# Decoder layer: low halves of wz in the last attention group made by GpSimd, x2 sums moved up on VectorE

## What is computed

```
b_att = softmax(max(s, axis=2), axis=1)
q2c_att = einsum('bc,bcd->bd', b_att, c)[:, None, :]
x = concatenate([c, c2q_att, c * c2q_att, c * q2c_att], axis=-1)
z = x @ W_l.T + b_l
```

## Time and profile before

| what | number |
|---|---|
| median of 3 runs | 656.0 us |
| profiled execution, its own time | 655.94 us |
| its span in the profile | 654.1 us |
| PE busy | 645.0 us (99%) |
| DVE busy | 470.1 us (72%) |
| ACT busy | 329.7 us (50%) |
| POOL busy | 241.3 us (37%) |
| mean granted clock of TensorE | 1.0 |

### The profile page before, as it was taken

One profiled execution on the slowest core, in us unless ns is written; L12 is line 12 of the kernel. 1 busy time (PEld: TensorE's weight loads), 2 busy tenths in 40 slices (PEclk: granted clock), 3 DMA queues, 4 the chain that ended last, 5 costly groups with the idle time before them and its releaser, 6 DMA issues. The chain is left out here.

```text
span 654.1 us, 11891 instructions
## 1 busy us (share of the span) xinstructions
PE 645.0 (99%) x3922; PEld 551.8 (84%) x3922; DVE 470.1 (72%) x1259; ACT 329.7 (50%) x779; POOL 241.3 (37%) x305
## 2 busy tenths in 40 slices
PE   8999999999999999999999989999999999999997
PEld 5878888889788888897897878888888888888887
DVE  5788868878788788787888978676575765747433
ACT  4575675555756755556576454333533344334331
POOL 2256163353562633534644233223232232322221
PEclk9999999999999999999999999999999999999999
DMA  8534044051340440513624260403214033230300
GB/s 232 155 97 144 8 124 122 28 168 48 92 145 7 122 122 25 165 54 87 197 71 125 84 220 21 180 27 130 98 52 174 0 129 96 70 125 1 151 13 32
DMA packets 51806, 64.44 MB, mean 99 GB/s; under 512 B 3944, under 2 KB 49560, under 8 KB 50880
## 3 DMA queue, kind: packets, MB, share of 16 engines
q1 hardware_dynamic: 51776, 64.06, 31.5%
HBM read 56.60 MB, written 7.45 MB: 98 GB/s over the span
## 5 line engine op out<-in xcount | busy, mean ns | idle before, releaser
L1630 POOL TENSOR_TENSOR xt<-xt,cw_wide 128x512 f32<-128x512 f32 x55 | 72.5, 1318 | 187.2 <-ACT xt L1587 187.2
L1654 DVE TENSOR_TENSOR res<-bank,xt 128x512 f32<-128x512 f32 x62 | 42.6, 688 | 62.3 <-POOL xt L1630 58.3
L1591 ACT ACTIVATE a_hi<-res 128x512 fp32r<-128x512 f32 x42 | 26.7, 635 | 82.4 <-DVE res L1654 82.4
L75 PE MATMUL bank<-h_hi,w_lo 128*128 128x512 f32 x168 | 67.1, 400 | 0.1
L76 PE MATMUL bank<-h_lo,w_hi 128*128 128x512 f32 x168 | 65.9, 392 | 0.0
L77 PE MATMUL bank<-h_hi,w_hi 128*128 128x512 f32 x168 | 65.6, 390 | 0.0
L1025 POOL TENSOR_TENSOR wz_lo<-tmp,wz_hi 128x512 fp32r<-128x512 f32 x28 | 34.9, 1284 | 37.6 <-DVE tmp L1196 37.6
L643 PE MATMUL bank<-cw_wide,ctw 128*112 128x375 f32 x128 | 46.7, 486 | 0.4
L656 PE MATMUL bank<-ctxf,qg 125*112 125x256 f32 x192 | 46.7, 379 | 0.0
L1659 DVE TENSOR_TENSOR a_lo<-res,a_hi 128x512 fp32r<-128x512 f32 x42 | 30.0, 714 | 22.4 <-ACT a_hi L1591 22.4
L1587 ACT ACTIVATE xt<-bank 128x512 f32<-128x512 f32 x61 | 36.0, 590 | 14.6 <-PE bank L77 14.5
(11 more groups left out here) (241 smaller groups left out, 2016.1 us busy)
## 6 DMA issues: line engine op xcount, KB each, us to landing
cw_wide<-in_ctx_t SPq DMA_DIRECT2D x32, 375.0 KB
ctxf<-in_ctx SPq DMA_DIRECT2D x32, 375.0 KB
cw_wide<-cw_scratch SPq DMA_DIRECT2D x7, 1536.0 KB, 7.5
xt<-in_x SPq DMA_DIRECT2D x8, 448.0 KB, 3.9
x_scratch<-x2b SPq DMA_DIRECT2D x8, 448.0 KB, 3.2
x2n<-x_scratch SPq DMA_DIRECT2D x7, 512.0 KB, 4.6
cw_wide<-cw_scratch SPq DMA_DIRECT2D x7, 512.0 KB, 4.2
x2t<-x_scratch SPq DMA_DIRECT2D x7, 512.0 KB, 3.9
```

Source lines behind the costliest of these rows:

```text
L75: pe.matmul(dst, a_lo, b_hi, start=first, stop=False, **kw)
L1591: act.activation(a_hi[n % (AHEAD + 1)][:, :], af[(p + n) % 2][:, :], ACT.Copy).then_inc(a_hi_ok, 1)
L1630: pool.tensor_tensor(sg[b][:, :], sg[b][:, :], cw_wide[p][:, ORDER[n], :], ALU.mult).then_inc(sgw_ok, 1)
L1654: dve.tensor_tensor(af[b][:, :], u_bank[b][:, :], sg[b][:, :], ALU.mult).then_inc(af_ok, 1)
```

## The change

In the last attention group the four subtractions `wz_lo[j] = wz[j] - wz_hi[j]` go from VectorE to GpSimd. GpSimd makes each as soon as its high half is there, without waiting for all sums, and ahead of the weighting of `sg[1]`; the wait for `wz_lo_ok` falls away there, since GpSimd itself has made them. VectorE runs its four sums in a row, then the low half `op_lo0`, and then the two x2 sums; before, `op_lo0` stood behind the x2 sums.

```
@@ GpSimd, group @@
                     if last:
+                        for j in range(G):
+                            pool.wait_ge(wz_hi_ok, ev[j])
+                            pool.tensor_tensor(wz_lo[:, j, :, :], wz[:, j, :, :], f32(wz_hi[:, j, :, :]), ALU.subtract).then_inc(wz_lo_ok, 1)
                         pool.wait_ge(sg_ok, 2)
                         pool.wait_ge(cw_in, 16)
-                        pool.wait_ge(wz_lo_ok, ev[G - 1])
                         pool.tensor_tensor(sg[1][:, :], sg[1][:, :], cw_wide0[:, 0, :], ALU.mult).then_inc(sgw_ok, 1)
@@ VectorE, group @@
-                    def wz_low_last(j):
-                        dve.wait_ge(wz_hi_ok, ev[j])
-                        dve.tensor_tensor(wz_lo[:, j, :, :], wz[:, j, :, :], f32(wz_hi[:, j, :, :]), ALU.subtract).then_inc(wz_lo_ok, 1)
...
-                        wz_sum(0)
-                        wz_sum(1)
-                        wz_low_last(0)
-                        wz_sum(2)
-                        wz_low_last(1)
-                        wz_sum(3)
-                        wz_low_last(2)
-                        wz_low_last(3)
+                        for j in range(G):
+                            wz_sum(j)
+                        dve.wait_ge(a_hi_ok, 1)
+                        dve.tensor_tensor(op_lo0[:, :], af[0][:, :], f32(op_hi0[:, :]), ALU.subtract).then_inc(a_lo_ok, 1)
                         x2_sum(i, 0)
                         x2_sum(i, 1)
-                        dve.wait_ge(a_hi_ok, 1)
-                        dve.tensor_tensor(op_lo0[:, :], af[0][:, :], f32(op_hi0[:, :]), ALU.subtract).then_inc(a_lo_ok, 1)
```

## The result

The changed kernel takes 658.0 us (median of 10 runs), the one before 656.19 (10 runs beside it): ratio 1.0031, 95% interval 1.0022 to 1.0039. It is slower by 1.8 us; 658.2 was forecast. The profiled execution took 658.32 us, with a span of 656.5 against 654.1.

A forecast was written before the change was run, and what follows sets the result against it. The engines' meeting between the blocks, which VectorE reaches last, was taken as the bound. With turns VectorE arrives at 377.83 + 1.82 = 379.65 against 377.47, +2.2 us; 656.0 + 2.2 = 658.2, range 657.4 to 659.2.

The forecast's parts named there:

- The bound and the meeting: Between the two blocks, VectorE reaches the engines' meeting (L306) last; a meeting x later makes the kernel x longer.
- The tail of 1.82 us: Last group: six products and a VectorE instruction from last low half to last x2 sum take 1.82 us, unchanged.
- Part 1: Moving op_lo0 ahead of the x2 sums takes 0.59 us out of the tail before the meeting; all would be had.
- Part 2 and its cover: Low halves on GpSimd: meeting 0.2 us later at best, wait for routing weights covered; +2.2 us with contention.
- The turns: VectorE's sums and GpSimd's low halves, each reading two SBUF tiles, alternate, one standing still for the whole of the other.
- the sum: Last group with handovers of 1.15 and 0.35 us: VectorE at the meeting at 379.65 against 377.47, +2.2 us, 658.2.
- rival 3: Handovers with dead time, as the skill's 115 ns: three at a quarter of a microsecond, 658.9 us; chance 0.04.
- a change in the length of the part behind the meeting: Second block, TensorE's first product to the end: forecast unchanged in time; a change would mean the forecast is wrong.
- the clock term: TensorE in the last group: clock granted 1.00, no new pause longer than 1.5 us, so no time added for it.
- Rival 1: No contention between VectorE's sums and GpSimd's low halves: +0.2 us, 656.2; chance 0.11.
- Rival 2: Second block: the later meeting shifts coincidences, so `e_gt` and `choice` lose no 1.86 us; 654.3; chance 0.03.
- Rival 4: TensorE's clock falls as it waits for each low half; comes on top, past 659; chance 0.03.

The follow-up runs named there:

- e1: Kernel before with only op_lo0 moved ahead of the two x2 sums, low halves staying on VectorE: 655.66 us, ratio 0.9993 to the kernel before.
- e3: Changed kernel with the last group's eight wz sums taking their added operand from PSUM instead of SBUF: 656.61 us, ratio 1.0007 to the kernel before.
- e6: Kernel before with op_lo0 early and only the last low half given to GpSimd: 656.48 us, ratio 1.0002 to the kernel before.
- e5: Changed kernel with GpSimd starting its low halves only after all eight sums: 658.63 us, ratio 1.0038 to the kernel before.
- the second comparison: Changed kernel itself, unaltered, measured again beside the kernel before on the same chip: 658.36 us, ratio 1.0031.
- e4: Changed kernel with eleven products nobody reads filling TensorE's pauses: 658.04 us, ratio 1.0027 to the kernel before.
- e4b: Changed kernel with the eleven unread products in TensorE's pauses, measured once more beside the changed kernel: 658.11 us, ratio 1.0030 to the kernel before.
- e2: Changed kernel with op_lo0 put back behind the x2 sums, only the low halves moved to GpSimd: 659.01 us, ratio 1.0042 to the kernel before.

## Why the prediction was right, and where it was off

**The bound and the meeting: right.** The stage got 2.27 us longer and the end came 2.41 later. Where the clock stayed up, the second block took 272.3 us whatever the stage did (e1, e3 to e6), so a later meeting passes on one to one.

**The tail of 1.82 us: right while the clock is up.** e5: last low half 377.49, last x2 sum 379.31. In the changed kernel's profile it is 2.17 (377.30 to 379.47), because the last three of the six products of `z_c(3)`, and part of the one ahead of them, ran at the lower clock.

**Part 1: too high.** "All 0.59 would be had" took GpSimd's 376.85 as fixed. It hangs on a DMA that lands some tenths earlier or later; e1 had 0.2 in the profile and 0.5 in the median. In the changed kernel this doesn't count: the low halves hold GpSimd up beyond that DMA.

**Part 2 and its cover: right.** The turns came in the forecast order, with `op_lo0` in the hole before the last high half and the first x2 sum behind it; that one and the last low half overlap and keep their lengths (0.68 and 1.26 us). The price of a handover to GpSimd was 1.16, 1.15 and 1.14 us from VectorE's end to GpSimd's, against the 1.15 of the sum (the first counted with 0.48 us for sum 2's first half, printed from 370.53). The one back to VectorE was 0.28, 0.27 and 0.29 us against my 0.35, three times 0.07. That is nearly all of the 0.26 us by which the last low half came earlier than in the sum (8.36 us after the first sum, not 377.83 - 369.21 = 8.62). The Trainium skill ("SBUF — State Buffer", "Who interferes with whom") calls VectorE instructions with two SBUF inputs and GpSimd instructions that read SBUF exclusive: the trace agrees, for sums of 128x256 too (1.50 us for 0.48), and e3 shows that the second SBUF input is what does it (eight sums in 3.22 us). The dead time of rival 3 is not there.

**The sum.** 2.2 forecast, 1.8 in the medians beside each other, 2.3 in the second comparison. With the measured handovers and the clock up the stage would have grown by 8.36 + 1.82 + 0.33 - 8.59 = 1.92 us; the profile's 2.27 has 0.35 of lower clock in it. So the profile's +2.4 comes as near to the forecast's +2.2 as it does partly by luck: handovers priced 0.26 us too high and a first sum that came 0.27 us earlier stand against 0.35 and 0.41 us of lower clock that the sum had at nothing. The prediction named a change in the length of the part behind the meeting as a sign that it is wrong. That sign came, by 0.41 us, and it goes against the clock term, not against the turns: with the clock up in e4 and e4b that part has its old length.

**Rivals.** Rival 1 fell with the 1.50 us rows. Rival 2 did not come: `choice` and `e_gt` took 0.96 and 1.51 us in the changed kernel as before. Rival 4, the clock, was given 0.03 and came in part: it fell in both profiles, with mean clocks of 0.995, and 5 of 16 runs have that mean. The step that failed was the one from "Granted now is 1.00 even over the 1.7 us without a product" and "none of the new pauses is longer than 1.5 us" to a clock that stays up. The pauses were as short as said (1.33 us at most), and the clock fell. Nor does the busy time of the stretch tell by itself: TensorE was busy 2.94 of the 5.20 us from 372.5 to 377.7, just before the fall, against 3.42 of 5.30 us before its meeting in the kernel before. But in e5's profile it was busy only 3.85 of the 7.10 us from 372.5 to 379.6, with pauses of up to 1.50 us, and the clock stayed at 1.00. What beyond the pauses decides it stays open. And a single profile of the kernel before did not show its whole behaviour: 16 of its 43 runs beside the experiments have a mean clock of 0.997. The rival's price ("past 659") was too high for the median and for four of the five runs (658.32 to 658.85); one took 659.46.

## What to carry to other kernels

Before you give an elementwise step to an idle GpSimd, look at what VectorE does at that moment and how many SBUF inputs that has: with two on both sides the engines take turns, and each step puts most of its GpSimd length on VectorE's own path (here a sum of 0.48 us became 1.50 beside a low half of 1.28). In the other groups of the kernel before GpSimd's work comes after the sums, and its list of waits has nobody who waits for it; at the end of a block the wait is open. If one operand of VectorE's step can come from PSUM, the contention goes (e3). Of this change only the move of `op_lo0` is worth keeping, and even its half microsecond is at the edge of what the runs can tell.

## What the runs showed of the hardware that was not expected

TensorE's granted clock fell to half with no pause longer than 1.33 us: in the changed kernel at about 377.7 us, after three pauses of 0.46, 0.46 and 1.33 us from 373.2 us on (TensorE's rows above), and it came back only some 7 us later, though TensorE was busy without a break from 379.80 on. The same program shows it in some executions and not in others. By the chain of the kernel before, TensorE doesn't set the pace right behind the meeting; in the changed kernel it does, and it stands still for 0.9 us of the second block against 2.1 before. That is probably why the 4.6 us from 379.80 to 384.4 at half the clock cost the second block only 0.2 to 0.4 us in the two profiles of the changed kernel (0.8 in e2).
